# A graph kernel's second attention loop: adding gathered rows in PSUM with an identity product, and one VectorE operation for relu and product

## The reference

```python
x_l = x @ W_l
x_r = x @ W_r
e = jax.nn.leaky_relu(x_l[src] + x_r[dst], NEG_SLOPE) @ att     # NEG_SLOPE = 0.2
e_max = jax.ops.segment_max(e, dst, num_segments=N)
e_exp = jnp.exp(e - e_max[dst])
denom = jax.ops.segment_sum(e_exp, dst, num_segments=N)
alpha = e_exp / denom[dst]
out = jax.ops.segment_sum(alpha[:, None] * x_l[src], dst, num_segments=N)
```

## Time and profile before

| | |
|---|---|
| median of three runs | 4830.54 us (4828.19 to 4831.01) |
| the profiled execution | 4824.61 us, its span 4822.8 us |
| VectorE busy | 2781.6 us (58%) |
| GpSimd busy | 2686.7 us (56%) |
| TensorE busy, products | 2356.4 us (49%) |
| second attention loop | from about 3106 to 4455 us of the span |

### The profile page before, as it was taken

One profiled execution on the slowest core, in us unless ns is written; L12 is line 12 of the kernel. 1 busy time (PEld: TensorE's weight loads), 2 busy tenths in 40 slices (PEclk: granted clock), 3 DMA queues, 4 the chain that ended last, 5 costly groups with the idle time before them and its releaser, 6 DMA issues. The chain is left out here.

```text
span 4822.8 us, 75928 instructions
## 1 busy us (share of the span) xinstructions
PE 2356.4 (49%) x18851; PEld 1736.9 (36%) x18904; DVE 2781.6 (58%) x5419; ACT 647.4 (13%) x1473; POOL 2686.7 (56%) x2730
## 2 busy tenths in 40 slices
PE   0133333333306624666666665355555555555798
PEld 0023333333305513454544454233333333333232
DVE  8641111111118865777777777577877887877201
ACT  0001111111105410111111111011111111111000
POOL 0037777777745522777777774176666666663000
PEclk9955555555555555566666656555555555555899
DMA  0133334343315523555555552143333333332744
GB/s 21 38 123 124 125 122 130 126 129 123 114 36 109 107 47 85 140 144 148 143 147 147 143 146 78 42 102 94 94 95 91 91 97 92 94 95 60 275 170 168
DMA packets 533005, 537.07 MB, mean 111 GB/s; under 512 B 213790, under 2 KB 370324, under 8 KB 532618
## 3 DMA queue, kind: packets, MB, share of 16 engines
q1 hardware_dynamic: 243738, 289.79, 20.1%
q0 software_dynamic: 81072, 115.39, 10.7%
q10 hardware_dynamic: 208000, 130.01, 8.8%
HBM read 376.99 MB, written 159.58 MB: 111 GB/s over the span
## 5 line engine op out<-in xcount | busy, mean ns | idle before, releaser
L1381 POOL DMA_INDIRECT rows<-nodes_xl,id_slot x832 | 868.3, 1044 | 577.8 <-issue 240.9
L638 POOL DMA_INDIRECT msg_by_src<-message,place_slot x832 | 832.6, 1001 | 343.5 <-issue 252.8
L1381 POOL DMA_INDIRECT rows<-nodes_kv,id_slot x832 | 822.6, 989 | 339.8 <-issue 242.0
L1697 PE MATMUL counts_p<-hot_blocks 128*128 128x128 bf16 x2080 | 541.1, 413 | 362.3 <-DVE running_counts L1569 319.8
L599 PE MATMUL picked<-X,hotT 128*128 x1664 | 374.5, 423 | 674.2 <-issue 390.3
L599 PEld LDWEIGHTS picked<-X,hotT 128*128 128x128 f32 x1664 | 360.6, 331 | 688.0 <-issue 688.0
L560 DVE TENSOR_TENSOR message<-picked,w_dst 128x512 f32<-128x512 f32 x104 | 71.9, 691 | 845.7 <-ACT message L612 838.0
L1738 PE MATMUL sums<-parts,hot 128*128 128x68 bf16 (+1 forms) x4992 | 325.2, 251 | 374.9 <-DVE parts L1558 374.9
L1697 PEld LDWEIGHTS counts_p<-hot_blocks 128*128 128x128 bf16 x2080 | 277.5, 148 | 545.0 <-DVE running_counts L1569 339.1
L1738 PEld LDWEIGHTS sums<-parts,hot 128*128 128x128 bf16 x4992 | 311.8, 168 | 424.1 <-issue 424.1
L1569 DVE SCALAR_TENSOR_TENSOR running_counts<-running_counts,same_block,counts_p 128x128 f32<-128x128 f32 x1040 | 359.8, 346 | 171.0 <-DVE running_counts L1569 31.3
(11 more groups left out here) (343 smaller groups left out, 3606.2 us busy)
## 6 DMA issues: line engine op xcount, KB each, us to landing
adjacency<-running_counts ACTq DMA_DIRECT2D x1040, 64.0 KB
loc_all<-loc_by_cell SPq DMA_DIRECT2D x104, 512.0 KB
hotT<-hotT_by_step SPq DMA_DIRECT2D x208, 256.0 KB, 3.1
hot<-hot_by_step SPq DMA_DIRECT2D x208, 256.0 KB, 3.1
blocks<-adjacency SPq DMA_DIRECT2D x40, 1280.0 KB, 11.4
hot_by_step<-hot ACTq DMA_DIRECT2D x104, 256.0 KB, 2.0
hotT_by_step<-hotT ACTq DMA_DIRECT2D x104, 256.0 KB, 2.2
rows<-msg_by_src SPq DMA_DIRECT2D x312, 68.0 KB
```

What stands on the lines that cost most here:

```text
L638: pool.indirect_dma_start(out=msg_dram, out_offset=bass.IndirectOffsetOnAxis(ap=ids[:, s, t:t + 1], axis=0), in_=rows[:, s, t, :], in_offs ...
L1381: pool.indirect_dma_start(out=rows[:, j, t, :], out_offset=None, in_=table, in_offset=bass.IndirectOffsetOnAxis(ap=ids[:, j, t:t + 1], axis=0)
L1697: ins = nc.tensor.matmul(counts_p[:, q - HALVES[half][0], :], hot_b[:, r, 1, :, t], hot_b[:, r, 0, :, t], start=g == 0, stop=g == 1)
```

## The change

In the second loop (`not ef`) `pick` begins with one product of the identity with the gathered rows of the step, 512 columns in f32, which starts the accumulation in `picked`; it waits for `arrived`. The 24 products with `near` now add to it. So `picked` holds x_l[src] + x_r[dst] when VectorE reads it.

The leaky relu of z is written as 0.2 z + 0.8 relu(z). `gat` computes relu and the product with 0.8 att in one operation, reduces, and adds 0.2 att . x_l[src], which each gathered row now carries as a 66th number. The part 0.2 att . x_r[dst] is the same for all edges of a destination and is left out, in the self loop's score too. The first loop's code is the same as before.

```diff
--- before.py
+++ after.py
@@ -1666,12 +1666,15 @@
                             pe.wait_ge(hotT_in[j % 4], (i * 2 + j // 4 + 1) * 16)
                             if not (isinstance(i, int) and J < 2):
                                 pe.wait_ge(scored, (J - 1) * score_steps)
+                            if not ef:
+                                pe.wait_ge(arrived[j], i * (16 * TB) + 16 * TB)
+                                nc.tensor.matmul(picked[:, j % 2, :, :], ident[:], rows[:, j, :, 0:D], start=True, stop=False)
                             for q, n in enumerate(ns):
                                 for g in range(2):
                                     t = 2 * q + g
                                     for m in range(3):
                                         ins = nc.tensor.matmul(picked[:, j % 2, t, :], hotT[:, j % 4, t, :], near[:, m, bass.ds(n, D)],
-                                                               start=m == 0, stop=m == 2)
+                                                               start=ef and m == 0, stop=m == 2 and (ef or t == TB - 1))
                             ins.then_inc(products, 1)
 
                         def add_bias(w, slot, use):
@@ -1894,7 +1897,7 @@
                         sp.dma_start(to[:], frm).then_inc(s, 16)
                     sp.wait_ge(s, 16 * (len(pairs) + 1))
 
-        nodes_dram = {k: dram(f"nodes_{k}", [NPAD, w]) for k, w in (("kv", 2 * D + HEADS), ("xl", D + 1))}
+        nodes_dram = {k: dram(f"nodes_{k}", [NPAD, w]) for k, w in (("kv", 2 * D + HEADS), ("xl", D + 2))}
 
         X = sbuf("X", [P, NT, D])
         block_row = sbuf("block_row", [1, BCELLS], I32)
@@ -2008,7 +2011,8 @@
 
         with ExitStack() as c:
             near = sbuf("xr_parts", [P, 3, 4 * 512], BF16, ctx=c)
-            xl = sbuf("xl", [P, NT, D + 1], ctx=c)
+            xl = sbuf("xl", [P, NT, D + 2], ctx=c)
+            att_r = sbuf("att_relu", [P, D], ctx=c)
             own_s = sbuf("own_score", [P, NT], ctx=c)
             with ExitStack() as c1:
                 lr = sbuf("lr", [P, NT, 2 * D], ctx=c1)
@@ -2016,26 +2020,29 @@
 
                 def own_scores(step, sq, a, b):
                     v = nc.vector
-                    step(v.memset(xl[:, :, D:], 1.0))
+                    step(v.memset(xl[:, :, D:D + 1], 1.0))
+                    step(v.tensor_scalar(att_r[:], att_s[:], 0.8, None, ALU.mult))
+                    step(v.tensor_tensor(sq[:], lr[:, :, 0:D], rowwise(att_s[:]), ALU.mult))
+                    step(v.tensor_reduce(a[:], sq[:], AX.X, ALU.add))
+                    step(v.tensor_scalar(xl[:, :, D + 1], a[:], 0.2, None, ALU.mult))
                     step(v.tensor_copy(xl[:, :, 0:D], lr[:, :, 0:D]))
                     step(v.tensor_tensor(sq[:], lr[:, :, 0:D], lr[:, :, D:2 * D], ALU.add))
-                    step(v.scalar_tensor_tensor(sq[:], sq[:], 0.2, sq[:], ALU.mult, ALU.max))
-                    step(v.tensor_tensor(sq[:], sq[:], rowwise(att_s[:]), ALU.mult))
+                    step(v.scalar_tensor_tensor(sq[:], sq[:], 0.0, rowwise(att_r[:]), ALU.max, ALU.mult))
                     step(v.tensor_reduce(own_s[:], sq[:], AX.X, ALU.add))
+                    step(v.tensor_tensor(own_s[:], own_s[:], xl[:, :, D + 1], ALU.add))
                     three_parts(step, lr[:, :, D:2 * D], near, sq)
                 node_math(own_scores, norms=0)
                 store([(node_view("xl"), xl[:])])
             c2 = ExitStack()
             product = sbuf("score_a", [P, TB, D], ctx=c2)
-            leaky = sbuf("score_b", [P, TB, D], ctx=c2)
 
             def gat(step, picked, rows, to):
                 v = nc.vector
-                step(v.tensor_tensor(product[:], picked, rows[:, :, 0:D], ALU.add))
-                step(v.scalar_tensor_tensor(leaky[:], product[:], 0.2, product[:], ALU.mult, ALU.max))
-                step(v.tensor_tensor(product[:], leaky[:], att_s[:].unsqueeze(1).to_broadcast([P, TB, D]), ALU.mult))
+                step(v.scalar_tensor_tensor(product[:], picked, 0.0, att_r[:].unsqueeze(1).to_broadcast([P, TB, D]),
+                                            ALU.max, ALU.mult))
                 step(v.tensor_reduce(to, product[:], AX.X, ALU.add))
-            attend(1, nodes_dram["xl"], D + 1, 0, D + 2, near, gat, 4, False, None, (BFIRST * STEPS, BSECOND), acc)
+                step(v.tensor_tensor(to, to, rows[:, :, D + 1], ALU.add))
+            attend(1, nodes_dram["xl"], D + 2, 0, D + 2, near, gat, 3, False, None, (BFIRST * STEPS, BSECOND), acc)
             c2.close()
             both = sbuf("both_exps", [P, 2, NT], ctx=c)
             most = sbuf("most", [P, NT], ctx=c)
```

## The result

The changed kernel takes 4714.74 us (median of four runs, 4713.69 to 4717.3) where the kernel before takes 4830.07: ratio 0.9762, 95% interval 0.9746 to 0.9779, or 115 us less. The forecast was 4727, with 4698 to 4762 as its range. The profiled execution took 4715.26 us, its span 4713.5, so the two spans are 109.3 us apart.

What follows compares the result with a forecast made beforehand. VectorE's chain was taken to set the step, 13.0 us each over 104 steps. Terms -130 + 8 + 16 + 2 = -104 us took the profiled 4824.6 to 4720.6; with 5.9 to the median, 4726.5, rounded 4727; range 4698 to 4762.

Steps and rivals of the forecast that it cites:

- Score: Second loop, VectorE: two large operations go and one small addition comes, 1.26 us a step, 130 us less over 104 steps.
- Identity product: TensorE, start of each pick: one added f32 product of 1.9 or 0.96 us, mostly covered; 8 us lost, bounds 0 and 22.
- step 3: Last step of a four-step window: counts 0.3 to 0.4 us late for VectorE at the lower clock, in time at the higher.
- step 4 of a round: Step 0 of every other window: turned scores some 0.9 us late for VectorE at the lower clock, 13 times.
- high-clock rival: TensorE's clock stays up in the loop: no product late, half of the 31 us carry-column wait goes; 4700, chance 0.10.
- The wait: Picks wait for gathered rows: cost 0 in mid-loop, 16 us once at the loop's start, bounds 8 and 25.
- Before the loop: Node operations ahead of the loop: one large operation net and 4 small ones more, 2 us added.
- low-clock rival: TensorE comes late at the lower clock: 22 us in place of 8, up to another 10; 4741 to 4751, chance 0.14.
- gathers' pace: Rival: GpSimd's gathers set the loop's pace; 2 us lost in each of 26 windows, 52 us, 4779; chance 0.10.
- slower case: Rival: the whole pick lies on the path in every step, each paying 1.9 and saving 1.26; 4915, chance 0.04.
- GpSimd's idle time before weighing: Sign in the new profile: POOL's idle time before weighing falls from 185 to some 60 us.
- VectorE's waits for TensorE's counts and turned scores: Sign in the new profile: these waits of VectorE for TensorE stay under 30 us.

Runs made afterwards that it cites:

- VectorE's part alone: The changed kernel without the identity product and its wait, with the old flags of the picks; 4707.43 us, ratio 0.9743 to the kernel before.

## Why the prediction was right, and what was mis-sized

- *Score, 130 us (1.26 a step).* Right: 1.27, by VectorE's part alone, and nearly the whole effect.
- *Identity product, 8 us lost.* This is the term that was mis-sized, and wrong in sign: 4 us were gained in steps 8 to 102. The product's length was right (2.05 and 1.04 against 1.9 and 0.96 for the two clocks). Of the two places where it was to come late, step 3 was not late, since the clock had risen before its product; step 4 of a round was late by 0.2 us in place of 0.9 (12 times), since the clock rose behind the product, in the picks. (By the prediction's own figures, 3666.4 against 3665.6, the 0.9 should have been 0.8.) What the prediction had not booked is step 1 of a window, where the higher clock shortens the carries: 0.25 us, 24 times. The high-clock rival named this place and put it at half of the 31 us. Against VectorE's part alone the wait fell by 5 of 35; against the kernel before it hardly fell at all (31.0 to 30.1), since with VectorE's part alone it had risen to 35.2. That rival had the clock fall a few us after TensorE stops, and the earlier trace rows don't show the fall. In that trace TensorE stopped at 3664.87 and the clock was 1.00 up to 3665.6 and 0.50 behind it:

```profile
3664.87:3665.60 0.73, 0.00 (x0) 0.00 (x0) 0.73 (x1) 0.00 (x0) 0.42 (x2) 1.00 1.07 385
3665.70:3667.70 2.00, 0.00 (x0) 0.00 (x0) 1.93 (x4) 0.20 (x1) 1.65 (x2) 0.50 0.84 233
```

- *The wait, nothing in the loop, 16 us at its start.* Right within 2 us. No pick waited for rows after the first round. At step 6 the changed kernel was 8.9 us late by the start of its loop, forecast 10. The whole charge is what remains of 104 x 1.26 = 131 and the gain of 4 when the measured 120.5 is taken off: 14.5 us. 11.2 of it is the product's wait (by the first 8 steps); the other 3 are there without the product too. That a faster VectorE meets the same gathers would explain them and wasn't tried.
- *Before the loop, 2 us.* 2.6: one large operation (1.8) and three small ones (the text first says three and then counts four).

Sum by these: -131 - 4 + 14.5 + 2.6 = -118, against a forecast of -104. It must agree with the two profiles, since the 14.5 is a remainder. The medians are 115 apart; the 3 us between are no more than executions of one kernel differ (4713.69 to 4717.3), and the profiled execution of the kernel before was itself 5.5 below its median. So of the 14 us by which the sum of the terms was off, 12 are the identity product. The low-clock rival, the gathers' pace and the slower case did not happen at the usual speed.

Of the signs, the durations, the rising clock (0.67 in the loop, by the view below) and the late start came as said. Two did not: GpSimd's idle time before weighing fell to 82 and not to 60 us, and VectorE's waits for TensorE's counts and turned scores were over 30 us (49.1 for the counts alone), because of the start.

```profile
3114.00:4352.00 1238.00, 828.32 (x6994) 530.46 (x7020) 954.61 (x2116) 171.20 (x393) 857.83 (x832) 0.67 0.40 101
```

## What to carry to other kernels

Work taken from the engine whose chain sets the length of a step counts in full as long as each other engine has room at the very place. Room is read step by step, not from a mean: TensorE was busy in about half of the time, and yet a second product cost 0.6 to 1.0 us at step 1 of a window and nothing at step 2. An instruction with a wait holds up all that stands behind it in its engine's order, and this costs where its data are last to arrive, here at the start of the loop. Moving it back helped only as far as the gathers' lead reached, so after such a repair look for the step that pays it back. And when a trace holds the same step at two levels of the clock, compare the two before building an experiment.

## What the runs showed of the hardware beyond expectation

More TensorE work made other TensorE work shorter. With 190 us of products added to the kernel with VectorE's part alone, a record of the carry product fell from 358 to 283 ns, one of the opening of the sums from 634 to 473, and the picks' busy time in the loop from 152.9 to 126.8 us. The counts (128 columns with a load of weights before each) hardly gained, 413 to 411 ns. Within one trace the carry product (two records) took 0.58 us at a granted clock of 0.50 and 0.38 us at 1.00.

One set of runs took 6.2 ms in place of 4.7, for every kernel in it, with VectorE's score operations as long as before and only the waits longer.
